# Long feature-by-feature scans with multipliers in PSUM, in both layers of a graph network kernel

## The reference

```python
# layer 0, 4 heads of 16
h = (x @ W_node).reshape(n, H, HD)
attn = a_src_node[src] + a_dst_node[dst] + edge_attr @ W_edge
attn = jnp.where(attn >= 0, attn, 0.2 * attn)
attn = jnp.exp(attn - attn_max[dst])          # maximum over each dst
attn = attn / (attn_sum[dst] + 1e-8)
out = zeros.at[dst].add(h[src] * attn[:, :, None])
x = layernorm(x + layernorm(out + h) * gamma + beta)
# layer 1
h = relu(concatenate([x[src], x[dst], edge_attr]) @ W1 + b1)
aggregated = segment_sum(h @ W2 + b2, dst) / max(degree, 1)
x = layernorm(x + aggregated + x @ Wn + bn)
```

## Time and profile before

| | us |
|---|---|
| median of 3 runs | 4755.95 (4751.53 to 4757.55) |
| span of the profiled execution | 4755.7 |
| POOL busy | 3565.7 |
| DVE busy | 2619.7 |
| PE busy | 1308.6 |
| ACT busy | 493.5 |

### The profile page before, as it was taken

The page is one execution under the profiler, slowest core; times in us unless marked ns, Lnnn a source line. Parts: engine busy times, 40 slices in busy tenths (PEclk is TensorE's granted clock), DMA queues, the critical chain, the costliest instruction groups (busy, mean ns, idle before and its releaser), DMA issues. The chain is left out here.

```text
span 4755.7 us, 33914 instructions
## 1 busy us (share of the span) xinstructions
PE 1308.6 (28%) x3363; PEld 660.9 (14%) x3363; DVE 2619.7 (55%) x8568; ACT 493.5 (10%) x1011; POOL 3565.7 (75%) x3558
## 2 busy tenths in 40 slices
PE   7600000000000000000575333333333333333336
PEld 4300000000000000000453111111111111111126
DVE  6545443344433444433774666666666666666645
ACT  4500000000000000000232111111111111111101
POOL 5777777777777777777676777777777777777766
PEclk9855555555555555555555655655665556556655
DMA  3034333333333333333232555555555555555532
GB/s 124 10 112 160 100 105 118 118 117 112 93 118 118 118 118 99 106 118 113 85 121 94 169 171 167 165 170 170 162 170 171 161 170 171 166 166 171 170 104 63
DMA packets 240932, 622.28 MB, mean 131 GB/s; under 512 B 74956, under 2 KB 102543, under 8 KB 221521
## 3 DMA queue, kind: packets, MB, share of 16 engines
q1 hardware_dynamic: 127568, 443.81, 28.2%
q0 software_dynamic: 113280, 177.74, 14.7%
HBM read 328.11 MB, written 293.29 MB: 131 GB/s over the span
## 5 line engine op out<-in xcount | busy, mean ns | idle before, releaser
L525 POOL DMA_INDIRECT edge_arena<-table1s,ix x1568 | 1518.0, 968 | 477.9 <-issue 435.2
L433 POOL DMA_INDIRECT edge_arena<-table,ix x1440 | 1460.5, 1014 | 438.9 <-issue 438.9
L565 PE MATMUL ps<-w1e_bd,edge_terms 128*128 128x512 f32 x784 | 725.1, 1080 | 1264.4 <-DMA edge_terms<-e32g_d 1264.4
L1191 DVE SCALAR_TENSOR_TENSOR edge_arena<-edge_arena,same 128x128 f32<-128x128 f32 x1568 | 542.0, 346 | 263.6 <-issue 189.1
L565 PE MATMUL ps<-we_bd,edge_terms 128*128 128x32 f32 x392 | 93.6, 403 | 1864.1 <-DVE score L1038 1803.8
L1035 DVE TENSOR_TENSOR score<-edge_arena,node_wide 128x128 f32<-128x128 f32 x49 | 14.2, 291 | 1066.0 <-DMA edge_arena<-table,ix 1065.6
L1057 DVE TENSOR_TENSOR_SCAN edge_arena<-wq,edge_arena 128x32 f32<-128x32 f32 x3136 | 586.8, 268 | 1.8
L1197 DVE SCALAR_TENSOR_TENSOR edge_arena<-edge_arena,same 128x128 f32<-128x128 f32 x1568 | 539.7, 344 | 1.5 <-ACT edge_arena L832 1.2
L565 PEld LDWEIGHTS ps<-w1e_bd,edge_terms 128*128 128x128 f32 x784 | 229.0, 322 | 1759.2 <-issue 1759.2
L1209 DVE TENSOR_TENSOR edge_arena<-edge_arena 128x1024 f32<-128x1024 f32 x196 | 240.9, 1229 | 404.5 <-DMA edge_arena<-table1s,ix 404.5
L832 ACT ACTIVATE edge_arena<-edge_arena 128x1024 f32<-128x1024 f32 x196 | 207.0, 1056 | 1800.9 <-DVE edge_arena L1214 1800.9
(11 more groups left out here) (177 smaller groups left out, 1462.5 us busy)
## 6 DMA issues: line engine op xcount, KB each, us to landing
recv_term<-zeros SPq DMA_DIRECT2D x98, 1024.0 KB, 9.1
edge_arena<-recv_term SPq DMA_DIRECT2D x196, 512.0 KB, 4.1
rows<-edge_arena SPq DMA_DIRECT2D x196, 512.0 KB, 5.1
rows<-edge_arena SPq DMA_DIRECT2D x49, 1152.0 KB, 4.4
edge_arena<-table,ix POOLq DMA_INDIRECT x1568
edge_terms<-e32g_d SPq DMA_DIRECT2D x196, 128.0 KB, 4.8
edge_arena<-table1s,ix POOLq DMA_INDIRECT x1568
edge_terms<-e16g_d SPq DMA_DIRECT2D x49, 256.0 KB, 9.2
```

The source lines that it names most:

```text
L433: pool.indirect_dma_start(G0[slot][:, u, :], None, table0, bass.IndirectOffsetOnAxis(ap=ix[slot][:, u:u + 1], axis=0)).then_inc(gathered0[ ...
L525: pool.indirect_dma_start(G1[slot][:, u, :], None, table1s, bass.IndirectOffsetOnAxis(ap=ix[slot][:, u:u + 1], axis=0)).then_inc(gathered1 ...
L565: return pe.matmul(out_, lhsT, rhs, start=start, stop=stop)
L1191: stt(X[:, u, :], X[:, u - 1, :] if u else Xb[:, C1 - 1, :], same[:, bass.ds(c * C1 + u, 1)], X[:, u, :], ALU.mult, ALU.add).then_inc(dv1, 1)
```

## The change

Layer 0. The state of a chunk is laid out feature by feature in `F0`: 4 heads of 16 features and the weight sum, each with 33 places, of which the first holds the state at the end of the chunk before. The multipliers `decay` have the same layout, with 0 in the first place of each feature, and lie in PSUM, written by an ACT exponential of a broadcast argument (after.py L808). One scan of 2244 elements (L1172) does the work of the 68. The running maximum is one scan of 132 elements, with multipliers `hold0` in SBUF (L1157). The cut of the decay is a minimum with `cut` (0 or -1000) before the exponential. The weights lie in PSUM too, and the product (L1167) reads them there and writes into `F0`. ACT copies the sums, edge by edge again, into `R0` (L816 to L818). POOL's wait for a free buffer is on `g0_free`, counted behind the product.

Layer 1. C1 = 16, so there are 98 chunks. ACT copies the loaded receiver rows `X1` (now one buffer) feature by feature into `F1` and writes the relu there too; `hold1` (0 or 1, 30 features of 17 places) lies in PSUM. A scan of `F1` is four instructions of 510 elements and one of 136 (L1293), once for the receiver rows and once for the sums. PE adds the scanned receiver rows to the edge terms in PSUM by a matmul with the identity as stationary operand; DVE then adds the whole to `G1` in two instructions of 1024 elements with one operand in PSUM (L1325), and the addition at L1209 is gone. `F1` and `X1` lie in `node_arena`, so POOL and SP wait for `arena_free` before they load there. ACT copies the sums back edge by edge into `H1`.

The diff, cut:

```diff
-C1 = 8
+C1 = 16
...
+        HF = HD + 1
+        F0 = [part(node_arena, r * H * HF * T0, H * HF * T0) for r in range(2)]
+        F0_h = [f.rearrange("p (h d t) -> p h d t", d=HF, t=T0) for f in F0]
+        ps_flat = ps[:, :, :].rearrange("p a b -> p (a b)")
+        decay = ps_flat[:, 2 * BANK:2 * BANK + H * HF * T0]
+        decay_h = decay.rearrange("p (h d t) -> p h d t", d=HF, t=T0)
+        weight = ps[:, 7, 0:H * C0].rearrange("p (h t) -> p h t", t=C0)
+        cut = part(node_arena, 9296, LANE)
...
+        T1 = C1 + 1
+        F1 = [part(node_arena, i * HID * T1, HID * T1) for i in range(4)]
+        F1_f = [f.rearrange("p (f t) -> p f t", t=T1) for f in F1]
+        XF1, HF1 = (0, 1), (2, 3)
+        X1 = part(node_arena, 4 * HID * T1, C1, HID)
+        lead = part(node_arena, 4 * HID * T1 + W1R, HID)
+        FEATS = BANK // T1
+        hold1 = [ps[:, r, 0:FEATS * T1] for r in range(2)]
+        hold1_f = [h.rearrange("p (f t) -> p f t", t=T1) for h in hold1]
+        PIECES1 = [(f * T1, min(HID, f + FEATS) * T1) for f in range(0, HID, FEATS)]
...
+            def chunk1(c, s, loads=True, follows=True, stores=True):
+                if follows:
+                    sp.wait_ge(xf_ready, c + 1)
+                    sp.dma_start(X1, recv_p[:, bass.ds(c * C1 + C1, C1), :]).then_inc(recv_in, 16)
                 if loads:
...
+                    sp.wait_ge(edge1_mm, c * 2 + 4)
+                    sp.dma_start(edge_terms[s][:, :, :], e32g[:, bass.ds(c * 4 + 4 * RING1, 4), :]).then_inc(e32_in[s], 16)
+                if stores:
+                    store1(c - 1, 1 - s % 2)
...
-                    pool.wait_ge(rows0_ready, free_turn)
+                    pool.wait_ge(g0_free, free_turn)
...
+            pool.wait_ge(arena_free, 1)
...
             def edge1(c, s, it):
+                r = s % 2
                 pe.wait_ge(e32_in[s], it * 16 + 16)
...
+                for g in range(4):
+                    if g % 2 == 0:
+                        pe.wait_ge(half_used[g // 2], c + 1)
+                    mm(ps[:, 2 + g, :], edge_terms[s][:, g, :], w1e_bd[:, :], True, False)
+                pe.wait_ge(scanned_x, c + 1)
+                for g in range(4):
+                    recv = F1_f[XF1[r]][:, :, 1 + 4 * g:5 + 4 * g].rearrange("p f t -> p t f")
+                    last = mm(ps[:, 2 + g, :].rearrange("p (t f) -> p t f", f=HID), ident[:, :], recv, False, True)
+                    if g % 2:
+                        last.then_inc(edge1_mm, 1)
...
+            def hold(c, par):
+                act.activation(hold0[par][:, :, 1:T0], same[:, bass.ds(c * C0, C0)].unsqueeze(1).to_broadcast([P, H, C0]),
+                               ACT.Copy).then_inc(hold0_ready, 1)
+            def turn0(c, slot, copies, holds):
+                par = slot % 2
+                heads = lambda a: a.rearrange("p t (h d) -> p h d t", d=HD)
+                act.wait_ge(weight_arg, c + 1)
+                act.activation(weight, expo[:, 0, :, :], ACT.Exp).then_inc(weights_ready, 1)
+                act.wait_ge(rows0_ready, c + 1)
+                act.activation(F0_h[par][:, :, HD, 1:T0], expo[:, 0, :, :], ACT.Exp)
+                act.wait_ge(decay_arg, c + 1)
+                act.wait_ge(scanned0, c + 1)
+                act.activation(decay_h[:, :, :, 1:T0], expo[:, 1, :, :].unsqueeze(2).to_broadcast([P, H, HF, C0]),
+                               ACT.Exp).then_inc(decay_ready, 1)
                 if copies:
                     ix_copy(slot, bass.ds(c * C0 + RING0 * C0, C0), C0, ix0_ready)
...
+                if holds:
+                    hold(c + 2, par)
+                act.wait_ge(scanned0, c + 2)
+                act.wait_ge(rows0_stored[par], (c - par) * 8 + 16)
+                act.activation(heads(R0[par][:, :, 0:D]), F0_h[par][:, :, 0:HD, 1:T0], ACT.Copy)
+                act.activation(R0[par][:, :, ZCOL:MCOL].rearrange("p t h -> p h t"), F0_h[par][:, :, HD, 1:T0], ACT.Copy)
+                act.activation(R0[par][:, :, MCOL:ROW].rearrange("p t h -> p h t"), peak[par][:, :, 1:T0],
+                               ACT.Copy).then_inc(rows0_ready, 1)
...
+            def hold_1(c, r):
+                act.activation(hold1_f[r][:, :, 1:T1], same[:, bass.ds(c * C1, C1)].unsqueeze(1).to_broadcast([P, FEATS, C1]),
+                               ACT.Copy).then_inc(hold1_ready, 1)
+            def recv_1(c, r):
+                act.wait_ge(recv_in, c * 16 + 16)
+                act.activation(F1_f[XF1[r]][:, :, 1:T1].rearrange("p f t -> p t f"), X1, ACT.Copy).then_inc(xf_ready, 1)
+            def rows_1(c, r):
+                act.wait_ge(scanned1, c + 2)
+                act.wait_ge(rows1_stored[r], (c - r) * 8 + 16)
+                act.activation(H1[r], F1_f[HF1[r]][:, :, 1:T1].rearrange("p f t -> p t f"), ACT.Copy).then_inc(rows1_ready, 1)
+            def turn1(c, s, copies=True, follows=True, c_later=True):
+                r = s % 2
+                if follows:
+                    act.wait_ge(led_x, c + 1)
+                    act.wait_ge(edge1_mm, c * 2 + 2)
+                    recv_1(c + 1, 1 - r)
+                if c_later:
+                    rows_1(c - 1, 1 - r)
+                    if follows:
+                        hold_1(c + 1, 1 - r)
+                for h in range(2):
+                    act.wait_ge(half_used[h], c + 2)
+                if c_later:
+                    act.wait_ge(rows1_ready, c)
+                act.activation(F1_f[HF1[r]][:, :, 1:T1].rearrange("p f t -> p t f"), G1[s], ACT.Relu).then_inc(relu_done, 1)
                 if copies:
...
+            link(ts(cut, same[:, :], 1.0, CUT, ALU.subtract, ALU.mult))
...
+                G, F, M, Mb = G0[slot], F0_h[par], peak[par], peak[1 - par]
+                now = score[:, :, 1:T0]
+                now_t = now.rearrange("p h t -> p t h")
                 dve.wait_ge(gathered0[slot], it * (16 * C0) + 16 * C0)
...
+                tt(now_t, G[:, :, D:D + H], terms[:, bass.ds(c * C0, C0), :], ALU.add)
+                dve.tensor_copy(score[:, :, 0:1], Mb[:, :, C0:T0]).then_inc(dv0, 1)
+                dve.wait_ge(dv0, c * STEPS_T + 1)
                 dve.wait_ge(edge_mm, c + 1)
...
+                tt(now_t, now_t, ps[:, par, 0:C0 * H].rearrange("p (t h) -> p t h", h=H), ALU.add).then_inc(edge_mm_free, 1)
                 dve.wait_ge(edge_mm_free, c + 3)
...
+                stt(now, now, SLOPE, now, ALU.mult, ALU.max).then_inc(dv0, 1)
+                dve.wait_ge(dv0, c * STEPS_T + 2)
+                dve.wait_ge(hold0_ready, c + 1)
                 dve.wait_ge(rows0_ready, c + 1)
...
+                flat = lambda a: a[:, :, :].rearrange("p h t -> p (h t)")
+                scan(flat(M), flat(hold0[par]), flat(score), 0.0, ALU.mult, ALU.max).then_inc(dv0, 1)
+                dve.wait_ge(dv0, c * STEPS_T + 3)
+                tt(expo[:, 0, :, :], now, M[:, :, 1:T0], ALU.subtract).then_inc(weight_arg, 1)
+                tt(expo[:, 1, :, :], M[:, :, 0:C0], M[:, :, 1:T0], ALU.subtract).then_inc(dv0, 1)
+                dve.wait_ge(dv0, c * STEPS_T + 4)
+                tt(expo[:, 1, :, :], expo[:, 1, :, :], wide(cut[:, bass.ds(c * C0, C0)].unsqueeze(1), [P, H, C0]),
+                   ALU.min).then_inc(decay_arg, 1)
+                dve.wait_ge(scanned0, c + 1)
+                dve.tensor_copy(F[:, :, :, 0:1], F0_h[1 - par][:, :, :, C0:T0]).then_inc(dv0, 1)
+                dve.wait_ge(weights_ready, c + 1)
+                tt(F[:, :, 0:HD, 1:T0], G[:, :, 0:D].rearrange("p t (h d) -> p h d t", d=HD),
+                   wide(weight.unsqueeze(2), [P, H, HD, C0]), ALU.mult).then_inc(g0_free, 1)
+                dve.wait_ge(dv0, c * STEPS_T + 5)
+                dve.wait_ge(g0_free, c + 1)
+                dve.wait_ge(decay_ready, c + 1)
+                scan(F0[par], decay, F0[par], 0.0, ALU.mult, ALU.add).then_inc(scanned0, 1)
             with dve.Fori(0, K0 // RING0) as it:
                 for slot in range(RING0):
...
+            dve.sem_inc(arena_free, 1)
...
+            def scan1(F, hold, done):
+                for lo, hi in PIECES1:
+                    last = scan(F[:, lo:hi], hold[:, 0:hi - lo], F[:, lo:hi], 0.0, ALU.mult, ALU.add)
+                last.then_inc(done, 1)
+            def sums1(c, r):
+                dve.wait_ge(led_h, c + 1)
+                dve.wait_ge(relu_done, c + 1)
+                scan1(F1[HF1[r]], hold1[r], scanned1)
+            def lead1(c, r):
+                dve.wait_ge(scanned1, c + 1)
+                dve.tensor_copy(F1_f[HF1[r]][:, :, 0:1], F1_f[HF1[1 - r]][:, :, C1:T1]).then_inc(led_h, 1)
+            def turn1(c, s, it, first=False):
+                r = s % 2
+                if first:
+                    dve.tensor_copy(F1_f[XF1[0]][:, :, 0:1], lead.unsqueeze(2)).then_inc(led_x, 1)
+                else:
+                    dve.wait_ge(scanned_x, c)
+                    dve.tensor_copy(F1_f[XF1[r]][:, :, 0:1], F1_f[XF1[1 - r]][:, :, C1:T1]).then_inc(led_x, 1)
+                    lead1(c - 1, 1 - r)
```

(10 more changed lines are left out.)

204 lines of the change are left out of this document (81 added, 123 removed).

## The result

The changed kernel takes 4623.59 us (4622.59 to 4626.21, 4 runs) against 4754.67 us before (4751.53 to 4757.55, 4 runs): a ratio of 0.9728, 95% interval 0.9714 to 0.9741. The profiled execution has a span of 4623.4 us, 132.3 less than the 4755.7 of before.

The account below looks back on a forecast made before the run. The prediction took POOL's list of gathers to bound both edge loops. From 4755.7 us, its terms -97 - 5 - 5 + 0 - 35 + 6 = -136 gave 4620 us, with a range of 4604 to 4668.

Parts of the forecast that it names:

- What bounds: Both edge loops: each lasts as long as POOL's list of gathers; DVE savings count only if they shorten gathers.
- Layer 0, the loop: 1440 gathers of layer 0 lose a 102.3 us stall except 5 us from short instructions: 97 us saved.
- First 128 gathers: Gathers overlapping layer 0's chunks 0 to 2 lose their stall too: another -5 us.
- Layer 0, the end: POOL's 24.2 us standstill after layer 0 falls to 18.8: -5 us, between -6 and -1 with half-rate strided sides.
- Layer 1, the start: POOL and SP's new wait for `arena_free` is covered by 9 us of scatters: cost 0.
- Layer 1, the loop: 1568 gathers lose a 39 us stall; two new copies per chunk give back 4: 35 us saved.
- Layer 1, the loop's cover: Per 20.0 us chunk, DVE 13 us, ACT 7, PE 9 to 15, chain 16: POOL stays the bound, slack 4.
- Layer 1, the end: POOL's 12.0 us standstill after layer 1 grows to 18.2: 6 us lost, 10 with half-rate strided copies.
- Rival A: Long scans hold POOL in both layers despite PSUM multipliers: 205 us plus 196 us, giving 5021 us; chance 5%.
- Rival B: PE bounds layer 1 because identity matmuls with strided reads take twice as long: 402 us more, 5022 us; chance 5%.
- Rival C: Gather stalls in the loops go only in part, short instructions catching one per chunk: 4640 to 4670 us; chance 12%.
- Rival D: Gathers in both loops are slow for another reason, such as DMA traffic, and stay so: 4757 us; chance 2%.

Follow-up runs that it names:

- f1_before_wq_psum: Kernel before, only layer 0's weights and decays (product and short-scan multipliers) moved to PSUM, weight-sum scans on an SBUF copy: 4648.51 us, ratio 0.9777 to the kernel before.
- f3_contiguous_reads: Changed kernel with identity matmuls and ACT copies to and from adjacent elements, values in wrong places: 4617.07 us, ratio 0.9709 to the kernel before.
- e2_decay_sbuf: Changed kernel with the multipliers of layer 0's long scan in SBUF instead of PSUM, on a slower chip: 5354.13 us, ratio 0.9461 to the kernel before.
- g1: Repetition on another slower chip of the changed kernel with layer 0's long-scan multipliers in SBUF: 5336.69 us, ratio 0.946 to the kernel before.
- e1: Kernel before with only layer 0's weights and decays moved to PSUM, on a slower chip: 5707.31 us against 5648.93, ratio 1.0095.
- g3: Changed kernel with layer 0's product done twice per chunk, on a slower chip: 5331.27 us, ratio 0.9454 to the kernel before.

## Why the prediction was right

4620 was predicted, 4623.6 measured, in the range and with every term of the right sign. Measured less foreseen, the terms are off by -2.4, -0.6, +2.4, 0, -0.1 and +4.4 us in the order of the prediction's sum; the first three all but cancel, which is luck, and the end of layer 1 is what is left. Point by point:

- **What bounds.** Right. POOL's list is the time of both edge loops; in f1_before_wq_psum the DVE work stayed and the gain came, and DVE's 450 us less are in none of the terms but that of the end of layer 0, where one chunk of them counts.
- **Layer 0, the loop.** -97 foreseen, -99.4 measured; the residual stall is not the 5 us that the short instructions were given but about 3 (1361.1 + 438.8 = 1799.9 against 1797.1). Which instructions it belongs to wasn't tested. First 128 gathers: -5 and -5.6.
- **Layer 0, the end.** -5 foreseen, -2.6 measured, within the bounds of -6 and -1. The step that was off is the size of the copy and of the product: 2.1 us for 2048 elements was taken from a contiguous ACT instruction, and 2.3 for the product from its old form, which reads `G0` row by row. The new forms take 3.87 us (L816, whose write is turned) and 3.83 (L1167, which writes 32 adjacent places of `F0` and reads `G0` with 288 bytes between neighbours). f1_before_wq_psum shows that the PSUM operand isn't what costs: there the product reads it too, row by row, and takes 2.28 us.
- **Layer 1, the start.** 0 foreseen and measured: no wait at the lead gather.
- **Layer 1, the loop.** -35 and -35.1. What is left of the stall, 1482.9 + 477.8 - 1957 = 3.7 us, agrees with the 4 us that the two copies of a chunk were given; that it is theirs, and that the 39 us of before were those of the 16 steps and L1209, is argued from their operands, since no run moved only these. The converse ran: `hold1` back in SBUF lengthens the gathers of layer 1 from 947 to 1176 ns.
- **Layer 1, the loop's cover.** ACT's copies of 2048 were put at 2.1 us here too, 7 us of ACT in a chunk. They take 3.83, and ACT is busy 1064.8 of 1800 us from 2600 on, 11.8 us in each 20. It fitted, so the mistake shows only at the ends.
- **Layer 1, the end.** +6 foreseen, +10.4 measured, just past the bound of +10: relu and copy at 3.83 us in place of 2.1 each (+3.4), landing 2.6 in place of 1.7 (+0.9). The half rate of strided sides was held as a bound of both ends, where it should have been the value: 8 us was priced, and 2.4 + 4.4 us came. f3_contiguous_reads shows it for a read (L912) and a write (L816); the strided writes at L907 and L928 only by their durations.
- **Rival A** is refuted by the trace itself: scans with a PSUM operand hold no gather, in 49 chunks and 98 chunks (the longest gather of the two loops takes 1135 and 1047 ns). Its price was nearly right: in e2_decay_sbuf the hold is 4.0 us in the chunk shown, where 4.2 was put.
- **Rival B.** The slow reads are real, the price wasn't reached. Identity matmuls take 0.94 us a record over the layer, and 7.4 us for about eight in the stretch above; the point from which PE would decide was 1.4 us. PE's chain lies inside the 20 us of POOL: DVE waits for the gathers' landing (750 us), not for PE. Of the two readings, "such a burst raises the clock" was the one that held: the granted clock in layer 1 rose from 0.58 to 0.78, with PE busy 1148.75 of 1800 us in place of 695.35 of 1900. The Trainium skill (page "SBUF — State Buffer", section on door 1) states a penalty for reads that go to another 16-byte line each time, without a size; the trace agrees, with 0.94 us a record against 0.72 for adjacent elements. Since only the size decides, the sentence of the prediction that by this rule the case would be the outcome doesn't follow from it.
- **Rival C.** Not seen; the stalls left in both loops are together 7 us at most.
- **Rival D** is refuted by f1_before_wq_psum.

The rule of the Trainium skill (page "SBUF — State Buffer", section "SBUF: two separate sides") that a DVE instruction with two SBUF inputs and a GpSimd instruction that reads SBUF exclude each other is borne out in both directions: by a mean of 944 ns in f1 with one operand moved away, and by a gather of 4.95 us in e2 with one moved back.

## What to carry to other kernels

When the bounding engine is GpSimd and its DMA commands have a mean above their median, look at which DVE instructions overlap the long ones and where their two inputs lie. Moving one small multiplier to PSUM was worth 106 us of 132, without any rewriting; do that first, then look for the few large SBUF-and-SBUF instructions outside the loop (another 22 us). The cost of a new layout shows at the ends of a stage, where nothing hides a copy: price a turned read or write of ACT at twice the contiguous one. And repeat the kernel before beside each group of variants: on the slower chips here the holds were in the trace and not in the time.

## What the runs showed of the hardware

- A scan with its multipliers in PSUM and its data in SBUF doesn't hold GpSimd's gathers; the same scan with both in SBUF holds one to its end (at most 0.95 us in the changed kernel, 3.5 to 5.5 us in e2 and g1, in each of 48 chunks).
- The place of the multipliers doesn't change the scan's own time: 4.83 us for 2244 elements either way.
- ACT copies 2048 fp32 elements in 1.91 us when contiguous and in 3.81 to 3.87 us when one side has 68 or 288 bytes between neighbours, be it the read (L912) or the write (L816). The DVE product of 2048 elements with one operand in PSUM takes 2.28 us when it reads the other row by row (f1), and 3.83 us when it reads it with 288 bytes between neighbours.
- A record of a matmul (half of one, 512 fp32 columns) with 68 bytes between the moving operand's neighbours takes 0.92 us at the upper clock, as long as a contiguous one at the lower (0.94, granted clock 0.50 in that stretch), and about twice a contiguous one at the upper (0.46).
- Chips differ: the kernel before takes 4755 us on one and 5640 and 5649 us on two others. There short DVE scans (e1) and gathers (g3) start 1.40 us apart in some stretches, with no releaser but issue, and run at full pace in others.
